# A graph kernel's edge weights as three rounded passes in place of plain fp32

## What is computed

```python
h = edge_feats                                   # 40000 x 8
for W in (W_mlp1, W_mlp2, W_mlp3):               # 8 -> 64 -> 64 -> 64
    h = SILU_2MOM * silu(h @ W / sqrt(W.shape[0]))
tpw = h @ W_mlp4 / sqrt(64)                      # 40000 x 512, the edge weights
w1, w2, w3, w4 = split(tpw, 4)
s0, s1 = x0[sender], x1[sender]                  # gathered sender rows, 128 and 3 x 128
p1 = w1 * s0 * y0
p2 = w2 * s0 * y1
p3 = w3 * s1 * y0
p4 = w4 * sum_m(s1 * y1) / sqrt(3)
msg = segment_sum(p, receiver)
```

## Time and profile before

| | |
|---|---|
| median of 3 executions | 1437.94 us (1435.26 to 1441.78) |
| span of the profiled execution, first to last instruction | 1589.5 us |
| granted TensorE clock, mean over the span | 0.968 |
| loop of the edge block in the profiled execution | some 612 of the 1589.5 us |

### The profile page before, as it was taken

One profiled execution on the slowest core, in us unless ns is written; L12 is line 12 of the kernel. 1 busy time (PEld: TensorE's weight loads), 2 busy tenths in 40 slices (PEclk: granted clock), 3 DMA queues, 4 the chain that ended last, 5 costly groups with the idle time before them and its releaser, 6 DMA issues.

```text
span 1589.5 us, 24654 instructions
## 1 busy us (share of the span) xinstructions
PE 1419.4 (89%) x8774; PEld 848.8 (53%) x8774; DVE 1163.6 (73%) x1635; ACT 994.4 (63%) x2000; POOL 916.9 (58%) x762
## 2 busy tenths in 40 slices
PE   5938999998999999999969888888888889888998
PEld 3626748883788568865743333333333333334887
DVE  7887729991899469964966777776778767675655
ACT  6347638881788468855745666776667766664443
POOL 4145658888888888888345555555556555553000
PEclk9868999999999999999999999999999999999999
DMA  9356392768267764654366777776777767765431
GB/s 329 121 208 195 106 382 56 265 212 307 38 249 274 234 209 145 213 174 113 57 212 196 231 222 232 236 231 213 232 232 242 236 209 235 227 205 183 147 107 53
DMA packets 91603, 316.56 MB, mean 199 GB/s; under 512 B 23754, under 2 KB 25988, under 8 KB 80859
## 3 DMA queue, kind: packets, MB, share of 16 engines
q1 hardware_dynamic: 45832, 202.57, 34.1%
q0 software_dynamic: 45648, 112.41, 27.6%
HBM read 378.96 MB, written 77.16 MB: 287 GB/s over the span
## 4 chain that ended last, share of the span: by engine, by line
PE 67%; DVE 20%; issue 6%; ACT 2%; another core or an unknown queue 2%; DMA 2%; DVEq 0%; SPq 0%; POOL 0%; ACTq 0%; POOLq 0%
PE pair L1599 29%; DVE arena L1049 10%; PE pair L1741 9%; PE pair L1636 5%; PE pair L1761 4%; DVE arena L1044 3%; PE pair L1855 3%; PE pair L1866 3%; PE pair L1653 3%; PE pair L1758 2%; PE pair L1590 2%; PE pair L1703 1%; PE pair L1807 1%; ACT arena L1227 1%
## 5 line engine op out<-in xcount | busy, mean ns | idle before, releaser
L1916 POOL DMA_INDIRECT sorted_edges<-arena x311 | 460.7, 1481 | 108.8 <-issue 95.4
L1953 POOL DMA_INDIRECT arena<-node_table,arena x352 | 336.5, 956 | 278.1 <-DVE arena L1049 178.7
L910 DVE TENSOR_TENSOR weights_hl<-arena,weights_hl 128x1024 fp32r<-128x1024 f32 x342 | 405.4, 1223 | 63.4 <-ACT weights_hl L1242 58.6
L1242 ACT ACTIVATE weights_hl<-arena 128x1024 fp32r<-128x1024 f32 x342 | 352.0, 1059 | 47.4 <-PE pair L1599 45.4
L1599 PE MATMUL pair<-weights_hl,rows_hl 128*128 128x512 f32 x1368 | 328.0, 397 | 4.6 <-ACT weights_hl L1242 3.0
L1049 DVE TENSOR_TENSOR arena<-pair,arena 128x768 f32<-128x768 f32 x352 | 318.7, 947 | 0.0
L1599 PEld LDWEIGHTS pair<-weights_hl,rows_hl 128*128 128x128 f32 x1368 | 253.2, 189 | 70.7 <-DVE weights_hl L910 10.2
L1741 PE MATMUL pair<-arena 64*128 64x512 f32 x704 | 216.0, 655 | 57.7 <-DVE arena L1049 45.0
L1044 DVE TENSOR_TENSOR arena<-pair,arena 128x512 f32<-128x512 f32 x176 | 120.4, 684 | 163.8 <-PE pair L1741 113.6
L1403 ACT ACTIVATE arena<-pair 128x512 f32<-128x512 f32 x176 | 105.4, 599 | 109.1 <-remote 88.8
L1761 PE MATMUL pair<-arena 128*32 128x256 f32 x2112 | 154.2, 380 | 21.4 <-issue 16.2
(11 more groups left out here) (292 smaller groups left out, 1550.9 us busy)
## 6 DMA issues: line engine op xcount, KB each, us to landing
arena<-in_w SPq DMA_DIRECT2D x73, 2048.0 KB
arena<-in_w SPq DMA_DIRECT2D x85, 1024.0 KB
sums<-arena SPq DMA_DIRECT2D x88, 512.0 KB
other_down<-in_w SPq DMA_DIRECT2D x8, 1024.0 KB
arena<-in_v SPq DMA_DIRECT2D x16, 512.0 KB, 4.6
pair_rows<-arena SPq DMA_DIRECT2D x1, 5934.0 KB
arena<-pair_rows SPq DMA_DIRECT2D x23, 256.0 KB
arena<-node_table,arena POOLq DMA_INDIRECT x352
```

What stands on the lines that cost most here:

```text
L910: v.tensor_tensor(out=part[s][:, 1], in0=by_chunk(n)[4], in1=part[s][:, 0].bitcast(F32), op=ALU.subtract).then_inc(v_low, 1)
L1242: a.activation(out=part[s][:, 0], in_=cols, func=ACT.Copy).then_inc(a_high, 1)
L1916: g.indirect_dma_start(out=sorted_edges, out_offset=bass.IndirectOffsetOnAxis(ap=slot_i[:, j:j + 1], axis=0), in_=er[:, j, :], in_offset=N ...
L1953: g.indirect_dma_start(out=row, out_offset=None, in_=table, in_offset=bass.IndirectOffsetOnAxis(ap=senders[:, i:i + 1], axis=0)).then_inc( ...
```

## The change

The product of `weights_of` becomes three fp32r passes, each in the same two row halves (so six matmuls for two tiles in place of two fp32 ones). For that, ScalarE writes the last layer's result a second time, rounded (`h3_hl[..., 0]`), VectorE makes its low part (`h3_hl[..., 1]`, `low_hidden_of`) in every odd step between the two messages of the step, and the weights `m4_sb` are split once ahead of the loop. The rest merges some semaphores with one use each and moves no instruction.

```diff
+        h3_0, h3_1, m4_hl = phase_tensors(edge_hidden_hl0=(1024, F32R), edge_hidden_hl1=(1024, F32R),
+                                          edge_weights_hl=(1024, F32R))
+        h3_hl = [h.rearrange("p (s c) -> p s c", s=2) for h in (h3_0, h3_1)]
+        m4_hl = m4_hl.rearrange("p (s c) -> p s c", s=2)
...
 def vector(v):
...
             v.wait_ge(p_part, begun[FT])
             v.wait_ge(d_late, 64)
+            v.wait_ge(a_high, ALONE * NCH + 1)
+            v.tensor_tensor(out=m4_hl[:, 1], in0=m4_sb, in1=m4_hl[:, 0].bitcast(F32),
+                            op=ALU.subtract).then_inc(v_low, 1)
             edge_tables()
...
+            def low_hidden_of(r):
+
+                v.wait_ge(a_mlp, mlp_place[r, 3] + 1)
+                v.tensor_tensor(out=h3_hl[r % 2][:, 1], in0=act3[r % 2], in1=h3_hl[r % 2][:, 0].bitcast(F32),
+                                op=ALU.subtract).then_inc(low_h3, 1)
...
             picks_of(0)
+            low_hidden_of(0)
             for s in range(STEPS):
...
                 messages_of(s, 0)
+                if s % 2 and s + 1 < STEPS:
+                    low_hidden_of(s // 2 + 1)
                 messages_of(s, 1)
...
 def scalar(a):
...
                 else:
+                    if r >= 2:
+                        a.wait_ge(low_h3, r - 1)
+                    a.activation(out=h3_hl[r % 2][:, 0].rearrange("p (h x) -> p h x", h=2), in_=b, func=ACT.Silu,
+                                 scale=SILU_2MOM / 8)
                     a.activation(out=act3[r % 2].rearrange("p (h x) -> p h x", h=2), in_=b, func=ACT.Silu,
                                  scale=SILU_2MOM / 8).then_inc(a_mlp, 1)
...
+            a.wait_ge(p_part, begun[FT])
+            a.wait_ge(d_late, 64)
+            a.activation(out=m4_hl[:, 0], in_=m4_sb, func=ACT.Copy).then_inc(a_high, 1)
             root(NORMS[0])
...
 def tensor(pe):
...
                 if i % BT == 0:
-                    pe.wait_ge(a_mlp, mlp_place[batch, 3] + 1)
+                    pe.wait_ge(low_h3, batch + 1)
+                if i == 0:
+                    pe.wait_ge(v_low, ALONE * NCH + 1)
                 if i >= Q:
                     pe.wait_ge(v_msg, i - Q + 2)
-                for h in range(2):
-                    p = slice(64 * h, 64 * (h + 1))
-                    mm = pe.matmul(out=tp_bank[(i + h) % Q], lhsT=act3[batch % 2][p, k * 128:(k + 1) * 128], rhs=m4_sb[p],
-                                   start=True, stop=True)
+                for a, b in PASSES:
+                    for h in range(2):
+                        p = slice(64 * h, 64 * (h + 1))
+                        mm = pe.matmul(out=tp_bank[(i + h) % Q], lhsT=h3_hl[batch % 2][p, a, k * 128:(k + 1) * 128],
+                                       rhs=m4_hl[p, b], start=a + b == 0, stop=a == 1, skip_group_check=True)
                 mm.then_inc(p_tp, 1)
```

More of the change, by code:

```diff
@@ L376, in program @@
         x_blank, fill_set, small_set = sem("x_blank"), sem("fill_set"), sem("small_set")
-        v_insub, v_key, v_hit, v_leaf, v_ids, v_eps, v_norm = (sem(n) for n in (
-            "in_sub_made", "limits_made", "limits_passed", "leaf_found", "ids_known", "eps_added", "normed"))
+        v_search, v_hit, v_leaf, v_ids, v_eps, v_norm = (sem(n) for n in (
+            "search_inputs_made", "limits_passed", "leaf_found", "ids_known", "eps_added", "normed"))
         v_scale, v_bounds, v_member, v_across, v_xseg, v_rowtot, v_starts, v_slots = (sem(n) for n in (
@@ L388, in program @@
         p_turn, p_logit, p_before = sem("turned_up"), sem("logits"), sem("counted_before")
-        v_picked, v_pairs, v_tiles, v_gap, v_route = (sem(n) for n in (
-            "picked", "pairs_known", "tiles_known", "gap_known", "routed"))
+        v_picked, v_pairs, v_tiles, v_route = (sem(n) for n in (
+            "picked", "pairs_known", "tiles_known", "gap_and_weights_known"))
         a_high, v_low, p_part = sem("weights_high"), sem("weights_low"), sem("weights_used")
@@ L399, in program @@
         a_pick, a_mlp = sem("last_picks_made"), sem("mlp_activated")
+        low_h3 = sem("edge_hidden_low")
         a_sum, a_kept = sem("sums_copied"), sem("sums_kept")
@@ L665, in vector @@
             T.did(v.scalar_tensor_tensor(out=in_sub, in0=K["node"], scalar=hi_p, in1=lowq,
-                                         op0=ALU.is_lt, op1=ALU.mult), v_insub, 1)
+                                         op0=ALU.is_lt, op1=ALU.mult), v_search, 1)
             v.wait_ge(a_mids, 2)
@@ L688, in vector @@
             T.did(v.tensor_tensor_scan(out=limit, data0=least, data1=least, initial=2 * BIG, op0=ALU.min,
-                                       op1=ALU.min), v_key, 1)
+                                       op1=ALU.min), v_search, 2)
             def tree_ids(b, n):
@@ L797, in vector @@
                     T.wait()
-                    T.did(v.tensor_tensor(out=gap2, in0=top2, in1=top1, op=ALU.subtract), v_gap, 1)
+                    T.did(v.tensor_tensor(out=gap2, in0=top2, in1=top1, op=ALU.subtract), v_route, 1)
                 T.wait()
@@ L821, in vector @@
             T.wait()
-            T.did(v.tensor_tensor(out=wt[1], in0=wt[0], in1=gap2, op=ALU.mult), v_route, 1)
+            T.did(v.tensor_tensor(out=wt[1], in0=wt[0], in1=gap2, op=ALU.mult), v_route, 2)
             v.wait_ge(p_before, 1)
@@ L1218, in scalar @@
             copy_turned(NT - 1)
-            a.wait_ge(v_gap, 1)
+            a.wait_ge(v_route, 1)
             a.activation(out=gap2, in_=gap2, func=ACT.Exp).then_inc(a_exp, 1)
@@ L1473, in spin @@
                     pe.matmul(out=bank[:, :], lhsT=ident, rhs=K["node"][:, 0:512], start=True, stop=True)
-            pe.wait_ge(v_insub, 1)
+            pe.wait_ge(v_search, 1)
             for t in range(NT):
@@ L1479, in tensor @@
             mm.then_inc(p_first, 1)
-            pe.wait_ge(v_key, 1)
+            pe.wait_ge(v_search, 2)
             def id_rows_of(tiles):
@@ L1899, in gpsimd @@
             g.wait_ge(g_rec, 5)
-            g.wait_ge(v_route, 1)
+            g.wait_ge(v_route, 2)
             g.wait_ge(v_pairs, 2)
```

## The result

| | before | changed |
|---|---|---|
| median, us | 1438.68 (4 executions, 1435.26 to 1441.78) | 1456.28 (4 executions, 1453.51 to 1458.69) |
| ratio | | 1.012, 95% interval 1.0086 to 1.0154 |
| span of the profiled execution | 1589.5 | 1456.7 |

A forecast was written before the change was run, and what follows sets the result against it. VectorE's own work was taken to fill 98% of the timed loop. Low part +26.8, waits that go -7, ahead of the loop +1 gave +20.8, rounded to +20 on 1437.9: 1458 us, range 1440 to 1474.

The forecast's parts named there:

- VectorE sets the loop: Rival 3, the forecast itself: VectorE's own work fills 98% of the timed loop; 1450 to 1468 us, chance 0.63.
- the sum: Forecast total: +26.8 for VectorE's low part, -7 for waits that go, +1 ahead of the loop, +20.8 us.
- What TensorE's gain gives back: In the loop, TensorE's faster calls remove VectorE's waits for it: at most 8 us, 7 taken.
- A call of `weights_of`: TensorE's edge weights' product in the loop: from 0.97 to 0.82 us per call, 26 us over 176 calls.
- Rival 4: Row halves of `weights_of` no longer side by side: 1.54 us per call, 1536 us, chance 0.05; milder case 1475, chance 0.06.
- The rule of the Trainium skill: Emptying PSUM may become the bottleneck when TensorE gets faster: nothing of TensorE's 26 us gained, time 1465 us.
- ScalarE: Last layer's function twice, 44 x 0.59 = 26 us in the loop: costs nothing while its 9% idle lasts.
- Ahead of the loop: Weights' split makes tables 2.0 us later, covered by a 1.97 us memory wait; with the first low part, 1 us.
- I take the stops to be the profile's own cost of records, and the 151.6 to lie in the loop: Profiled execution's 151.6 us excess over the timed median comes from recording in the loop; timed loop 460.4 us.
- the expected growth of the span by 20 to 45 us: Profiled span of the changed kernel grows, by more than the median, from added records at 18.3 per us.
- a loop whose span falls: Listed among signs in the changed kernel's profile that would show the forecast wrong.
- rival 1: TensorE sets the timed loop, which is above 487 us; the change makes the kernel faster, 1425 us; chance 0.12.

The follow-up runs named there:

- the runs with stops: Groups of runs in which the unchanged kernel, timed beside the others, took 1594 to 1596 us; a stop is TensorE standing still with nothing to wait for, or VectorE waiting over 2 us.
- the earlier trace: Profile of the unchanged kernel from which the forecast was made, taken with stops: span 1589.5 us.
- the fp32 kernel with all companions: Changed kernel with the product left in plain fp32, high and low parts made but unused: 1465.10 us, ratio 1.0169 without stops; 1572.25 us, 0.9848 with.
- The kernel with no low part: Changed kernel with low parts of hidden rows filled once ahead of the loop, all six matmuls kept: 1436.42 us, ratio 0.9979 without stops; 1610.11 us, 1.0106 with.
- that with SyncE's records: Kernel before with six register loads per step added on SyncE, 18 records more: 1440.36 us, ratio 1.0009, span 1437.9, without stops.
- the first and the fourth group: Two groups of runs on the same chip; the unchanged kernel took 1593.71 us in the first, with stops, and 1439.96 us in the fourth, without.

## Why the prediction was right, and where its reasons were not

**VectorE sets the loop: shown.** Without stops the low part and its companions add 491.3 - 465.7 = 25.6 us to the loop with fp32, and 484.1 - 460.1 = 24.0 us with the passes; the sum had 26.8. VectorE's busy time grows by 25.1 to 25.4 each time. Of the 44 low parts 43 stand in the loop, 0.60 apart, which is 25.8; the first falls into a wait of VectorE ahead of the loop and costs nothing there, which the sum did not see. The third price of the same instruction is from the runs with stops: twice the low part is 623.0 - 601.4 = 21.6 us more loop, on another chip than the changed kernel.

**What TensorE's gain gives back: shown.** The passes bring 491.3 - 484.1 = 7.2 us with the low part and 465.7 - 460.1 = 5.6 without; the sum had 7. VectorE's idle time falls from 14.3 to 7.5, by 6.8. The forecast had 8 falling to 1: both ends some 6 too low. Most of this is the single wait in the second step, 4.5 and 5.2 us, which the sum did not have; without it the idle time falls from 9.8 to 2.3, by 7.5. The 1.8 that are left of the side before may come from fp32 calls of 0.99 to 1.13 us in undisturbed steps (two in 1048.59 to 1050.85), where the sum had 0.97; this was not tested. The loop before was thus 465.7, where the forecast had worked out 460.4. In the changed kernel VectorE has no wait over 0.15 us from 850 to 1300.

**A call of `weights_of`: shown.** 0.80 against a forecast of 0.82, 0.97 from the earlier trace rows. Six matmuls at the 0.24 of the earlier trace rows would be 1.44 one after the other, so the row halves run side by side; weight loads add no time that can be seen. Rival 4 is out, and the granted clock in the loop is 1.00. Of TensorE's gain, 176 x 0.17 = 30 us by the earlier trace rows and 33 by the 0.99 of the undisturbed trace, 6 to 7 reach the end of the loop. The rule of the Trainium skill that was weighed ("TensorEngine Tiling", PSUM Bottleneck), as the prediction applied it, had all of it lost; the trace agrees in kind, and the share that isn't lost is VectorE's waits for TensorE.

**ScalarE: shown to be free with stops** (1.0004). Without stops it was not tried alone; there the fp32 kernel with all companions has VectorE's 25.1 more busy time and 0.5 more waits, which leaves nothing for ScalarE to have cost. The kernel with no low part has ScalarE's second function too, and its loop is shorter than before.

**Ahead of the loop.** The cover worked as the step said. The split of the weights makes VectorE wait and starts the tables later; the statistics then start without a wait. VectorE's timeline of the changed kernel:

```profile
784.37 0.91 DVE L1005 MEMSET arena<- 128x1024 f32 x1 [0.28 <-DVE weights_hl L915]
786.97 0.69 DVE L1009 TENSOR_TENSOR edge_weights_hl<-arena,edge_weights_hl 128x512 fp32r<-128x512 f32 x1 [1.69 <-ACT edge_weights_hl L1380]
787.58 2.03 DVE L610 TENSOR_TENSOR arena<-arena 128x1800 f32<-128x1800 f32 x1
...
798.36 0.69 DVE L458 BATCH_NORM_STATS2 arena<-arena 128x6 f32<-128x512 f32 x1
...
832.81 0.69 DVE L1052 TENSOR_TENSOR arena<-pair,arena 128x512 f32<-128x512 f32 x1 [1.98 <-PE pair L1768]
```

And of the kernel before without stops (that with SyncE's records):

```profile
780.62 0.91 DVE L1000 MEMSET arena<- 128x1024 f32 x1 [0.28 <-DVE weights_hl L910]
781.88 2.04 DVE L605 TENSOR_TENSOR arena<-arena 128x1800 f32<-128x1800 f32 x1 [0.36 <-PE pair L1599]
...
794.52 0.69 DVE L453 BATCH_NORM_STATS2 arena<-arena 128x6 f32<-128x512 f32 x1 [1.93 <-DMA arena<-node_sums]
...
829.16 0.69 DVE L1044 TENSOR_TENSOR arena<-pair,arena 128x512 f32<-128x512 f32 x1 [7.83 <-PE pair L1741]
```

From the memset to the tables it is 3.21 against 1.26 us, 1.95 later, as the 2.0 of the step; the wait of 1.93 for memory is gone, and from the memset to the first message it is 48.44 against 48.54. The transition costs nothing, where the sum had +1. The first message is 3.65 later all the same, because the memset is 3.75 later: the experts before it ended later. Their code is unchanged, and in the two other kernels of the group the memset starts at 781.33 and 782.65, so I take this for the scatter of single executions and not for the change; it was not tested.

**The sum, redone for the two spans:** 3.65 (ahead) + 18.4 (loop) - 3.2 (what lies behind the last product's start: 139.8 against 143.0, unchanged code again) = 18.8, the difference of the spans, 1456.7 - 1437.9. The loop alone, 18.4, is the difference of the medians, 17.6, within their scatter. The sum of the forecast, 20.8, has 26.8 for the low part, where 24.0 to 25.6 were measured, and 1 ahead of the loop, where there was nothing.

**The step that failed** is the one that the forecast put as "I take the stops to be the profile's own cost of records, and the 151.6 to lie in the loop". The second half holds: with stops and without, the loop differs by 611.3 - 465.7 = 145.6 us, and ahead of it by 7.6. The first half is refuted twice. The unchanged kernel's timed executions in three groups take 1594 to 1596 us, so the 151.6 us are not what sets a profiled execution apart from a timed one. And without stops the changed kernel writes (4860 + 4860 + 674 + 1233 + 347) / 483 = 24.8 records per us, more than the 18.3 of the earlier trace rows that were said to cause them. So the expected growth of the span by 20 to 45 us was wrong, and "a loop whose span falls" came true, with another cause than rival 1: not TensorE's share of a timed loop, but a profile and timings taken under two conditions. Rival 1 is out without stops: there the semaphore that ends a call of `weights_of` comes 16 to 28 ns after the modelled end for all 176 calls, before and changed, so TensorE is no later than its records. With stops its sign comes true.

The forecast held because the condition of the timings had no stops. Setting the 151.6 us aside was right for these timings, and the reason given for it was not; so far it was luck. What was worked out for a loop without stops was right by its mechanism. Had the timings been taken with stops, the time of the change would have been 1578 beside 1594, and the forecast wrong.

**What stays open** is why the stops reverse the sign. With stops the change adds the same 25 us to VectorE's busy time but takes 34.9 of its idle time away (157.7 to 122.8) in place of 6.8. The passes are not what does it: without them it is a gain of 1.5%, and with them but without the low part a loss of 1.1%. Nor is it any added work of VectorE: the same low part behind the second messages is 1.3% slower than before. The table says where to look. With stops both parts of the change have the other sign: the low part and its companions make the loop 611.3 - 594.4 = 16.9 us shorter with fp32, and the passes make it 626.4 - 611.3 = 15.1 longer by themselves and 7.0 with the low part. Idle time of 116 to 123 us is found only in the three kernels that have the low part between VectorE's messages; in the others it is 153 to 172. And the waits over 2 us lie in even and odd steps alike before (19 and 19), but 40 of 41 in odd steps in the changed kernel. So what lowers the idle time is the low part in its place between the messages. No run here tells why, and no version was found that is faster in both conditions and computes the same: the one that is 0.2% faster without stops leaves out part of the sum.

## What to carry to other kernels

In this loop, where two engines are both busy for some 98%, making one of them faster returned only the waits between them (7 of 30 us), and every instruction given to the other was paid in full (24 to 26 us of 26). In such a loop, cost the second before the first. Moving the work to a third engine need not help: on GpSimd the subtraction slowed VectorE's picks by nearly as much as it had cost. Compare the profiled span with the timed executions before using the profile, and if they are as far apart as here (10%), take an unchanged kernel's profile and timings together before costing anything, because the sign of a 1% change depended here on what separates them. Divide a trace that is disturbed into busy time and idle time: here the busy sums of a disturbed trace predicted the undisturbed time within 2 us.

## What the runs showed of the hardware

One kernel on one chip took 1593.71 us (17 executions) and later 1439.96 us (19 executions), and not one in between; the two conditions last for a whole group of runs. The difference lies nearly all in the edge loop (611.3 and 465.7 us). With stops the DMA share there is 0.72 against 0.90, which is no more than the same bytes over a longer time (225 GB/s for 612 us, 294 for 462). The loop has some 40 waits of VectorE over 2 us, where the undisturbed one has one, that of the second step. Some stand in the middle of a sum of TensorE, as in the earlier trace rows. In others both engines stand still in turn. VectorE's row of one, from the changed kernel's run with stops, then TensorE's rows around it:

```profile
1040.08 0.69 DVE L1052 TENSOR_TENSOR arena<-pair,arena 128x512 f32<-128x512 f32 x1 [2.50 <-remote]
```

```profile
1035.92 0.96 PE L1768 MATMUL pair<-edge_weights_hl,edge_hidden_hl 64*128 64x512 f32 x6
...
1039.68 1.48 PE L1788 MATMUL pair<-arena 128*32 128x256 f32 x24
1043.15 0.99 PE L1768 MATMUL pair<-edge_weights_hl,edge_hidden_hl 64*128 64x512 f32 x6 [1.99 <-DVE edge_hidden_hl L1065]
```

The message product at 1040.08 reads what the call at 1035.92 made, whose modelled end is 1036.88: it starts 3.2 us later, after 2.50 of idle time. It could also have waited for its gathered rows, and "remote" in the row says only that no instruction was found near the last semaphore update. The semaphores in the trace settle that: in all 41 waits over 2 us of this loop the rows had landed 3.9 us or more before, and the last update, within 0.45 us of the start, is that of `weights_of`. In the kernel before it is the same for all 38, with 5.9 us. TensorE has gone on with its sums until 1041.16 and then waits 1.99 for what VectorE makes late. The Trainium skill says of these ends ("Perfetto Trace Analysis") that the profiler estimates a matmul's end and does not observe it; the rows can't tell whether the products ended late or the news of them came late. But it is something that only the traces with stops have: in them the trace shows the update within 0.1 us of the modelled end for 52 (before) and 54 (changed) of the 176 calls, without stops for all 176.

What the stops are was not settled. It is not the number of records (20.0 per us in the changed kernel with stops, 24.8 without) and not the chip alone, as the first and the fourth group ran on the same one. It is not a late gather. The granted clock is 0.92 in the changed kernel's loop with stops and 1.00 without, but 0.98 in that of before with stops, and in that loop it falls to the lower of its two levels 6 times, beside 38 long waits. One of these times comes right behind the stop of the earlier trace rows, from 1083 on (granted clock 0.50 from 1083 to 1086, 0.98 from 1079 to 1083). So a lower clock comes with some of the stops and doesn't make them.
